# The feed-forward's input copied and shifted by DMAs, and its first two groups normalised among the attention's last slots

## The chip, the cores and the metric

The kernel runs on one core of a Trainium2 chip, as one launch. A core has TensorE (matmuls and transposes), VectorE, ScalarE and GpSimd (elementwise work) and SyncE, called SP here, which issues the DMAs. Each engine works through its own queue in order and waits on semaphores. TensorE writes its results to PSUM, eight banks of 128 partitions x 512 numbers; everything else lies in SBUF. The metric is the device time of one execution in microseconds.

## The reference, cut to what matters

Two inputs of 16 batches x 128 tokens x 128 numbers go through four stages: a cross-attention, a mixture of experts, a second cross-attention, and then six layers of local attention with a feed-forward. The change is in those six layers. Both halves of a layer begin with the same shift: of each token's 128 numbers the second 64 are taken from the token before (zeros for token 0).

```python
def shift_tokens(t):
    a, s = jnp.split(t, 2, -1)
    s = jnp.pad(s, ((0, 0), (1, 0), (0, 0)))[:, :-1]
    return jnp.concatenate([a, s], -1)

def ffn_layer(x, g, bln, W1, b1, W2, b2):
    mu = x.mean(-1, keepdims=True)
    var = ((x - mu) ** 2).mean(-1, keepdims=True)
    xn = (x - mu) / jnp.sqrt(var + 1e-05) * g + bln
    hg = xn @ W1 + b1
    a, gate = jnp.split(hg, 2, -1)
    return a * jax.nn.gelu(gate, approximate=False) @ W2 + b2
# a layer:  y = y + attn_layer(shift_tokens(y));  y = y + ffn_layer(shift_tokens(y))
```

## The kernel before

**Layout.** Y holds the running activations in SBUF as 128 tokens (partitions) x 16 batches x 128. [...]

**The attention as a pipeline.** A layer's attention has 64 units, four for each of the 16 batches. Each engine runs a list of steps, and each step has a skew: in slot c it handles unit c minus the skew. `start` writes out the first slots, `steady` is a loop over eight slots at a time, and `finish(0)` to `finish(6)` write out the last seven (slot 64 to slot 70, called finish slot 0 to 6 here). On GpSimd a slot is l_norm and l_scale of unit c-4 and l_add of unit c-3, in the order norm, add, scale; it is the scale (L555) that makes a unit ready for TensorE's transposes (l_turn_qk, L835, unit c-4). On VectorE a slot is, in this order, the split of x, the peaks of unit c-5, the sum of squares of unit c-2 (L1607), the division of unit c-6 (L1630, L1632), the small maximum of unit c-2 (L1622), the residual that writes a batch of Y (L1640, unit c-7, every fourth slot) and the rotation of unit c-1 (L1593, L1597). On TensorE a slot is scores (L854, L862), transposes of l_qk (L835), probability times values (L882), the two projections (L818, L827), output (L902), transposes of o (L892), transposes of the probabilities (L845) and, every fourth slot, those of x (L808). The engines are tied only by the semaphores between steps, so one may be slots ahead of another.

**The feed-forward.** It works in four groups g of four batches and three chunks k of the 341 hidden numbers. For each group TensorE first shifts Y into PSUM bank 1 with two matmuls against an identity and a shifted identity (shift, L923 and L924). VectorE takes the statistics from that bank (stats, L1653 and L1658), GpSimd makes 1/sqrt(var + eps) from them with an addition and a power (rstd, L566 and L568) and adds the bias b2 to Y (L571). VectorE normalises into the one buffer f_n (norm, L1666), TensorE transposes it into bank 2 (turn, L932), and ScalarE scales it into f_nT (L1227). Then come the hidden steps, written hidden(g,k) (L948, L949), the gelu on ScalarE, the gated product on VectorE (L1676), and the output (L959) with its residual (L1683).

**The order around the hand-over** is written out by hand, per engine, in into_feed_forward and out_of_feed_forward. TensorE has shift(0) behind finish slot 1, turn(0) behind slot 3, hidden(0,0) behind slot 4, shift(1) behind slot 5 and hidden(0,1) behind slot 6; VectorE has stats(0) behind slot 1, norm(0) behind slot 3, stats(1) before slot 6 and norm(1) behind it; GpSimd does all of its attention slots and only then its part of group 0. The remaining turns and shifts stand between the hidden steps of the groups before them. Between layers, the next attention's first slots are mixed into group 2 and 3, from the transpose of x at L808 on.

**SP** issues the DMAs in one queue: for each unit pair four copies that move the values across partitions (move_values, L360), for each batch two copies that bring the next batch of Y, shifted, to xin (take_x, L367 and L368), and the weights of the next layer.

Of the kernel before, what the change touches and what calls it, by code (L numbers as in the profile page):

```python
# [90 lines left out]
def build(nc, t, out):  # L91
    with ExitStack() as ctx:
# [135 lines left out]
        f_mv = sb("f_mv", [128, 4, 2])  # L228
        f_rs = sb("f_rs", [128, 4])
        f_n = sb("f_n", [128, 4, D])  # L230
# [13 lines left out]
        ld_xin = [sem(f"ld_xin{k}") for k in range(2)]  # L244
        tables, scaled_q = sem("tables"), sem("scaled_q")
# [24 lines left out]
        f = stage_sems("f_", "xs stats stat pool_st rstd n_done turned nT_done hidden gelu_done h_done out_mm yb_done "  # L270
# [4 lines left out]
        def apart(eng):  # L275


            eng.sem_inc(passed[eng.engine], 1)

# [6 lines left out]
        def _(sp):  # L286
# [87 lines left out]

            def serve_layer(ly, last):
# [50 lines left out]
        def _(pool):  # L426
# [55 lines left out]
            drive(pool, [(1, m_sum)], B, 2, 1)  # L482

# [76 lines left out]
            def feed_forward(ly, *groups):  # L560
                fb = ly * 4
                for g in groups:
                    yg = Y[:, 4 * g:4 * g + 4, :]
                    pool.wait_ge(f["stat"], upto(0, fb + g + 1))
                    apart(pool)
                    pool.tensor_scalar(f_rs[:], f_mv[:, :, 1], LN_EPS, None, ALU.add).then_inc(f["pool_st"], 1)  # L566
                    pool.wait_ge(f["pool_st"], upto(0, fb + g + 1))
                    pool.tensor_tensor(f_rs[:], f_rs[:], minus_half[:, 0:4], ALU.pow).then_inc(f["rstd"], 1)  # L568

                    pool.wait_ge(f["xs"], upto(0, fb + g + 1))  # L570
                    pool.tensor_tensor(yg, yg, f_b2[:, None, :].broadcast_to([128, 4, D]),  # L571
                                       ALU.add).then_inc(f["yb_done"], 1)

            def into_feed_forward(ly, att):
# [24 lines left out]
        def _(pe):  # L599
# [310 lines left out]
            def feed_forward(ly):  # L910
# [3 lines left out]
                def f_shift(g):  # L914

                    v = bank[:, 1, :].rearrange("p (a n) -> p a n", a=4)
                    yg = Y[:, 4 * g:4 * g + 4, :]
                    pe.wait_ge(l["res_done"], upto(0, ly * B + 4 * g + 4))
                    if g == 0:
                        pe.wait_ge(l["v_done"], upto(ub, UNITS))  # L920
                    else:
                        pe.wait_ge(f["n_done"], upto(0, fb + g))
                    pe.matmul(v[:, :, 0:HALF], ident, yg[:, :, 0:HALF], start=True, stop=True)  # L923
                    pe.matmul(v[:, :, HALF:], shift_t, yg[:, :, HALF:], start=True, stop=True).then_inc(f["xs"], 1)  # L924

                def f_turn(g):
                    pe.wait_ge(f["n_done"], upto(0, fb + g + 1))
                    if g == 0:
                        pe.wait_ge(l["qkT_done"], upto(ub, UNITS))
                    pe.wait_ge(f["nT_done"], upto(0, fb + g))  # L930
                    for n in range(4):
                        ins = pe.transpose(bank[:, 2, n * 128:(n + 1) * 128], f_n[:, n], ident)  # L932
# [30 lines left out]
                return f_shift, f_turn, f_hidden, f_out  # L963

            def into_feed_forward(ly, att):
                shift, turn_n, hidden, _ = feed_forward(ly)
# [860 lines left out]
```

## Time and profile before

| | |
|---|---|
| median of 3 runs | 2300.74 us (2296.83 to 2302.52) |
| the profiled execution's own time | 2298.88 us |
| its span, first to last instruction | 2297.1 us |
| TensorE's mean granted clock | 0.98 of full speed |
| TensorE, VectorE, ScalarE, GpSimd busy | 2163.7, 1708.3, 1555.0, 1410.4 us |
| shift matmuls, L923 and L924 | 16.0 and 14.9 us busy in all |
| GpSimd's wait ahead of L566 | 168.3 us in all, on VectorE's f_mv |

The engines work at the same time, so these busy times overlap. Busy time of TensorE is that of matmuls in a pipeline and may overlap with itself. The profiled execution is one of many, and its times are the ones that the rows further down give.

### The profile page before, as it was taken

What the parts mean: (1) busy time and instruction counts of PE and PEld (TensorE: products, weight loads), DVE (VectorE), ACT (ScalarE), POOL (GpSimd) and SP (SyncE); (2) the same over time, 40 slices, a digit from 0 to 9 for tenths busy, and PEclk for the clock granted to TensorE, in tenths of its full rate; (3) what the DMA queues carried; (4) which work ended last, traced back from release to release, by engine and by line L of the source; (5) the groups of instructions that cost most, each with busy time, mean ns of one, the idle gap of its engine ahead of it and who ended that gap; (6) DMA issues with size and microseconds to landing.
All of it is one profiled execution on the core that took longest, in us unless ns stands there. A gap on an engine that the chain in (4) does not pass through costs nothing.

```text
span 2297.1 us, 104869 instructions
## 1 busy us (share of the span) xinstructions
PE 2163.7 (94%) x36357; PEld 1677.6 (73%) x36357; DVE 1708.3 (74%) x4617; ACT 1555.0 (68%) x5192; POOL 1410.4 (61%) x2639
## 2 busy tenths in 40 slices
PE   6999789998999989999899998999989999899998
PEld 4776267776888758887588875788857888578885
DVE  4777878886888758787578875778757877578874
ACT  3553545554888748887488884888848888478883
POOL 3442711112888728887288882888828888288881
PEclk9997999997999999999999999999999999999999
DMA  3000000001211102111021110311103111021110
GB/s 102 0 0 1 0 1 0 0 0 54 75 41 42 35 26 75 40 42 35 23 77 42 41 36 18 81 42 39 39 18 79 42 40 40 16 51 43 42 40 20
DMA packets 120016, 82.33 MB, mean 36 GB/s; under 512 B 50998, under 2 KB 112580, under 8 KB 119876
## 3 DMA queue, kind: packets, MB, share of 16 engines
q1 hardware_dynamic: 119876, 80.43, 13.5%
q8 instruction: 92, 1.51, 0.3%
q14 instruction: 48, 0.39, 0.1%
HBM read 21.94 MB, written 1.05 MB: 10 GB/s over the span
## 4 chain that ended last, share of the span: by engine, by line
PE 74%; issue 5%; DVE 4%; POOL 2%; ACT 1%; DVEq 0%; POOLq 0%; ACTq 0%
PE bank L818 14%; PE bank L835 9%; PE bank L902 7%; PE bank L882 6%; PE bank L862 6%; PE bank L827 6%; PE bank L892 4%; PE bank L845 4%; PE bank L757 2%; PE bank L854 2%; PE bank L746 2%; PE bank L949 2%; PE bank L948 2%; PE bank L605 2%; PE bank L959 1%
## 5 line engine op out<-in xcount | busy, mean ns | idle before, releaser
L534 POOL TENSOR_TENSOR l_qk<-l_rot 128x512 f32<-128x512 f32 x384 | 494.2, 1287 | 106.0 <-DVE l_rot L1597 58.8
L1593 DVE TENSOR_TENSOR l_rot<-bank,l_tab 128x512 f32<-128x512 f32 x384 | 265.0, 690 | 185.7 <-ACT l_sq L1194 185.1
L1210 ACT ACTIVATE l_qkT<-bank 128x512 f32<-128x512 f32 x384 | 229.6, 598 | 255.2 <-PE bank L835 255.2
L555 POOL TENSOR_TENSOR l_qk<-l_qk,l_rn 128x512 f32<-128x512 f32 x384 | 400.7, 1044 | 0.9
L1174 ACT ACTIVATE prob<-bank,peak 128x64 f32<-128x64 f32 x1536 | 353.9, 321 | 1.3 <-DVE peak L1615 1.3
L818 PE MATMUL bank<-w_high,xs_part 128*128 128x512 f32 x768 | 347.4, 452 | 6.0 <-DVE xs_part L1584 5.4
L1597 DVE TENSOR_TENSOR l_rot<-bank,l_tab 128x512 f32<-128x512 f32 x384 | 261.4, 681 | 0.0
L1607 DVE TENSOR_REDUCE l_ss<-l_sq 128x8 f32<-128x512 f32 x384 | 259.6, 676 | 0.2
L835 PE MATMUL bank<-const,l_qk 128*128 128x128 f32 x1536 | 252.9, 287 | 6.5 <-POOL l_qk L555 5.8
L1194 ACT ACTIVATE l_sq<-bank 128x512 f32<-128x512 f32 x384 | 236.0, 615 | 23.8 <-PE bank L818 16.0
L902 PE MATMUL bank<-l_wo,l_oT 128*128 128x128 f32 x1536 | 237.4, 277 | 0.0
L827 PE MATMUL bank<-w_high,xs_part 128*128 128x256 f32 x768 | 199.9, 283 | 11.6 <-issue 11.6
L902 PEld LDWEIGHTS bank<-l_wo,l_oT 128*128 128x128 f32 x1536 | 204.8, 191 | 3.3 <-issue 0.3
L835 PEld LDWEIGHTS bank<-const,l_qk 128*128 128x128 f32 x1536 | 161.9, 141 | 42.9 <-POOL l_qk L555 9.6
L818 PEld LDWEIGHTS bank<-w_high,xs_part 128*128 128x128 f32 x768 | 144.9, 189 | 63.9 <-DVE xs_part L1584 7.1
L882 PE MATMUL bank<-l_v,probT 64*32 64x65 f32 x4608 | 177.2, 223 | 10.0 <-ACT probT L1182 6.5
L439 POOL TENSOR_SCALAR ln_rs<-ln_mv 128x1 f32<-128x1 f32 (+1 forms) x64 | 14.5, 227 | 274.2 <-DVE ln_mv L1561 129.4
L1615 DVE TENSOR_REDUCE peak<-bank 128x4 f32<-128x256 f32 x384 | 160.0, 417 | 28.9 <-PE bank L862 27.3
L862 PE MATMUL bank<-l_qkT 64*32 64x64 f32 x12288 | 174.7, 222 | 0.0
L882 PEld LDWEIGHTS bank<-l_v,probT 64*32 64x32 f32 x4608 | 115.4, 106 | 79.1 <-issue 79.1
L1632 DVE TENSOR_TENSOR o<-bank,rsum 128x256 f32<-128x256 f32 x384 | 163.0, 424 | 13.3
L882 PE MATMUL bank<-stash,probT 64*32 64x65 f32 x7680 | 172.2, 223 | 0.0
(201 smaller groups left out, 5287.8 us busy)
## 6 DMA issues: line engine op xcount, KB each, us to landing
stash<-l_v SPq DMA_DIRECT2D x768, 65.0 KB, 2.0
early<-in_L_ffn_Wqkv_dram SPq DMA_DIRECT2D x36, 256.0 KB, 3.1
l_wo<-in_L_ffn_Wo_dram SPq DMA_DIRECT2D x6, 512.0 KB, 4.0
xin<-Y SPq DMA_DIRECT2D x96, 32.0 KB
xin<-Y SPq DMA_DIRECT2D x96, 31.8 KB
f_w<-in_L_ffn_W_dram SPq DMA_DIRECT2D x6, 341.0 KB
out_dram<-X SPq DMA_DIRECT2D x4, 256.0 KB, 2.3
f_w<-in_L_ffn_W_dram SPq DMA_DIRECT2D x6, 128.0 KB
```

The source lines that it names most:

```text
L534: pool.tensor_tensor(l_qk[:, k], l_rot[:, k, 0], l_rot[:, k, 1], ALU.add).then_inc(l["add_done"], 1)
L555: pool.tensor_tensor(v, v, l_rn[:, k, :, None].broadcast_to([128, 8, L_DIM]), ALU.mult).then_inc(l["qk_done"], 1)
L818: ins = pe.matmul(bank[:, 0, :].rearrange("p (q n) -> p q n", q=2), xs_part[:, part, j // 4], w[:, 0:2, 256 * g:256 * g + 256], start=n == ...
L827: ins = pe.matmul(bank[:, 1, 0:256], xs_part[:, part, j // 4], w[:, 2, 256 * g:256 * g + 256], start=n == 0, stop=n == 2)
L835: ins = pe.transpose(bank[:, 2, n * 128:(n + 1) * 128], l_qk[:, j % 2, n * 128:(n + 1) * 128], ident)
L862: ins = pe.matmul(bank[w * WINDOW:(w + 1) * WINDOW, 3 + r, BAND * p:BAND * (p + 1)], l_qkT[rows, j % 2, queries:queries + WINDOW], l_qkT[r ...
L882: ins = pe.matmul(bank[w * WINDOW:(w + 1) * WINDOW, 6 - p, at:at + L_DIM + 1], probT[rows, j % 2, 128 * r + w * WINDOW:128 * r + (w + 1) * ...
L902: ins = pe.matmul(bank[:, 7, 256:384], l_oT[:, j // 4, p], l_wo[:, p], start=p == 0, stop=p == 7, skip_group_check=True)
L1174: ins = act.activation(prob[:, k, n * BAND:(n + 1) * BAND], bank[:, 3 + r, p * BAND:(p + 1) * BAND], ACT.Exp, bias=peak[:, k, n:n + 1])
L1593: dve.tensor_tensor(l_rot[:, k, 0].rearrange("p (q h n) -> p q h n", q=2, h=4), bank[:, 0, :].rearrange("p (q h n) -> p q h n", q=2, h=4), ...
L1597: dve.tensor_tensor(l_rot[:, k, 1].rearrange("p (q h s n) -> p q h s n", q=2, h=4, s=2), bank[:, 0, :].rearrange("p (q h s n) -> p q h s n ...
L1607: dve.tensor_reduce(l_ss[:, k, :, 0], l_sq[:].rearrange("p (h n) -> p h n", n=L_DIM), AX.X, ALU.add)\
```

## The change

The shift moves from TensorE to DMAs. The experts' buffer m_xT, which is free by then, becomes f_x, a shifted copy of all 16 batches of Y. SP fills it with two copies for each group of four batches, one of the first 64 numbers and one of the last 64 into the partition below. The copies of groups 0 to 2 are issued once batch 11's residual is done, between the moves of batch 13 and of batch 14; those of group 3 after the last residual. Row 0 of the shifted half is set to zero once. Statistics and norm read f_x. The semaphore xs and the function f_shift are gone, and the bias, which overwrites Y, now waits for the copies.

f_n, f_mv and f_rs get a second buffer (f_n's lies in c_oT, free by then), and the transposes alternate between bank 1 and bank 2. The order changes on four engines: stats, rstd and norm of groups 0 and 1 stand among finish slots 0 to 3, both turns and both copies of them behind slots 2 and 3; stats and norm of groups 2 and 3 move one group earlier.

```diff
+            def take_feed_forward(ly, first, end):
+                sp.wait_ge(l["res_done"], upto(ly * B, end))
+                apart(sp)
+                for b in range(first, end, 4):
+                    four = slice(b, b + 4)
+                    sp.dma_start(f_x[:, four, 0:HALF], Y[:, four, 0:HALF]).then_inc(ld_fx[b // 12], 16)
+                    sp.dma_start(f_x[1:, four, HALF:], Y[0:S - 1, four, HALF:]).then_inc(ld_fx[b // 12], 16)
...
                         move_values(ly, 2 * i + k, k, 1)
+                take_feed_forward(ly, 0, 12)
                 for b in range(B - 2, B):
                     for q in range(2):
                         move_values(ly, b, b % 2, q)
+                take_feed_forward(ly, 12, 16)
... GpSimd
             def into_feed_forward(ly, att):
+                rstd_n, bias = feed_forward(ly)
                 att.steady()
-                att.finish(0, 1, 2, 3)
+                att.finish(0)
+                rstd_n(0)
+                att.finish(1)
+                rstd_n(1)
+                att.finish(2, 3)
                 pool.wait_ge(ld_fw, (ly + 1) * (16 * FW_DMAS))
-                feed_forward(ly, 0)
+                bias(0)
 
             def out_of_feed_forward(ly, nxt):
-                feed_forward(ly, 1, 2, 3)
+                rstd_n, bias = feed_forward(ly)
+                rstd_n(2)
+                bias(1)
+                rstd_n(3)
+                bias(2)
+                bias(3)
... TensorE
-                att.finish(0, 1)
-                shift(0)
-                att.finish(2, 3)
+                att.finish(0, 1, 2)
+                turn_n(0)
+                att.finish(3)
+                turn_n(1)
                 pe.wait_ge(ld_fw, (ly + 1) * (16 * FW_DMAS))
-                turn_n(0)
                 att.finish(4)
                 hidden(0, 0)
-                att.finish(5)
-                shift(1)
-                att.finish(6)
+                att.finish(5, 6)
                 hidden(0, 1)
...
-                    if g < 3:
+                    if 0 < g < 3:
                         turn_n(g + 1)
                     hidden(g, 2)
...
-                    if g < 2:
-                        shift(g + 2)
... ScalarE
-                att.finish(0, 1, 2, 3)
+                att.finish(0, 1, 2)
                 act.wait_ge(ld_fw, (ly + 1) * (16 * FW_DMAS))
                 copy_n(0)
+                att.finish(3)
+                copy_n(1)
                 att.finish(4, 5)
... VectorE
-                att.finish(0, 1)
+                att.finish(0)
                 stats(0)
-                att.finish(2, 3)
+                att.finish(1)
+                stats(1)
                 norm(0)
-                att.finish(4, 5)
+                att.finish(2)
+                norm(1)
+                att.finish(3, 4, 5)
                 dve.wait_ge(ld_fw, (ly + 1) * (16 * FW_DMAS))
                 gated(0, 0)
-                stats(1)
                 att.finish(6)
-                norm(1)
...
                 for g in range(4):
-                    if 0 < g < 3:
-                        stats(g + 1)
+                    if g < 2:
+                        stats(g + 2)
...
                     if g > 0:
                         gated(g, 0)
-                    if 0 < g < 3:
-                        norm(g + 1)
+                    if g < 2:
+                        norm(g + 2)
```

## Rows read from the trace of the kernel before

**Rows 1.** The page's totals: busy time, share of the span, instructions of each engine.

```profile
PE 2163.7 (94%) x36357; PEld 1677.6 (73%) x36357; DVE 1708.3 (74%) x4617; ACT 1555.0 (68%) x5192; POOL 1410.4 (61%) x2639
```

**Rows 2.** Windows: stretch, length, busy time by engine, granted clock, DMA share, GB/s.

```profile
780.00:790.00 10.00, 10.00 (x240) 8.31 (x218) 7.91 (x22) 8.07 (x31) 8.60 (x17) 1.00 0.11 28
...
800.00:810.00 10.00, 7.87 (x124) 5.48 (x125) 3.25 (x11) 5.13 (x13) 0.00 (x0) 0.83 0.01 2
```

**Rows 3.** Timeline of GpSimd: start, us, engine, line, operation, [idle before <- releaser].

```profile
786.84 0.20 POOL L541 TENSOR_TENSOR l_t<-l_s,l_y 128x8 f32<-128x8 f32 x1
...
789.34 1.05 POOL L555 TENSOR_TENSOR l_qk<-l_qk,l_rn 128x512 f32<-128x512 f32 x1
...
792.93 1.04 POOL L555 TENSOR_TENSOR l_qk<-l_qk,l_rn 128x512 f32<-128x512 f32 x1
...
813.17 1.04 POOL L568 TENSOR_TENSOR f_rs<-f_rs,minus_half 128x4 f32<-128x4 f32 x1
```

**Rows 4.** Timeline of VectorE, finish slots 0, 1 and 3.

```profile
790.60 0.68 DVE L1597 TENSOR_TENSOR l_rot<-bank,l_tab 128x512 f32<-128x512 f32 x1
...
792.14 0.18 DVE L1630 RECIPROCAL rsum<-bank 128x4 f32<-128x4 f32 x1
...
792.70 0.16 DVE L1622 TENSOR_REDUCE l_s<-l_ss 128x8 f32<-128x16 f32 x1
...
799.39 0.18 DVE L1630 RECIPROCAL rsum<-bank 128x4 f32<-128x4 f32 x1 [0.62 <-PE bank L882]
```

**Rows 5.** Timeline of TensorE, finish slots 1 to 4.

```profile
790.89 0.66 PE L835 MATMUL bank<-const,l_qk 128*128 128x128 f32 x4
...
794.80 0.66 PE L835 MATMUL bank<-const,l_qk 128*128 128x128 f32 x4
...
798.14 0.66 PE L835 MATMUL bank<-const,l_qk 128*128 128x128 f32 x4
...
801.41 0.63 PE L932 MATMUL bank<-const,f_n 128*128 128x128 f32 x4 [0.65 <-issue]
801.87 0.28 PE L854 MATMUL bank<-l_mask,cbf 128*128 128x128 bf16 x2
```

**Rows 6.** Timeline of TensorE, the second shift and what follows it.

```profile
810.04 0.60 PE L923 MATMUL bank<-Y,const 128*128 128x256 f32 x2
...
810.91 0.61 PE L902 MATMUL bank<-l_wo,l_oT 128*128 128x128 f32 x4
```

**Rows 7.** Timeline of TensorE from hidden(0,1) to the next layer's first matmul.

```profile
811.35 1.02 PE L948 MATMUL bank<-f_nT,f_w 128*128 128x512 f32 x2
...
815.74 0.65 PE L932 MATMUL bank<-const,f_n 128*128 128x128 f32 x4 [2.51 <-DVE f_n L1666]
...
818.81 1.02 PE L948 MATMUL bank<-f_nT,f_w 128*128 128x512 f32 x2
...
820.53 2.73 PE L959 MATMUL bank<-f_w,f_h 128*128 128x128 f32 x23
...
823.21 1.02 PE L948 MATMUL bank<-f_nT,f_w 128*128 128x512 f32 x2
...
837.54 0.27 PE L808 MATMUL bank<-const,xin 128*128 128x128 f32 x1
```

**Rows 8.** Timeline of VectorE, statistics and norm of the second group.

```profile
811.23 0.89 DVE L1653 BATCH_NORM_STATS2 f_st<-bank 128x6 f32<-128x128 f32 x4 [0.88 <-PE bank L924]
...
814.24 1.36 DVE L1666 TENSOR_SCALAR f_n<-bank,f_mv,f_rs 128x128 f32<-128x128 f32 x4 [1.42 <-POOL f_rs L568]
```

**Rows 9.** Timeline of TensorE in the last layer: unit 61's transposes, and hidden(3,0).

```profile
2236.06 0.66 PE L835 MATMUL bank<-const,l_qk 128*128 128x128 f32 x4
...
2280.30 1.02 PE L948 MATMUL bank<-f_nT,f_w 128*128 128x512 f32 x2
```

**Rows 10.** SP's issues of L367: duration in ns, least, median, most.

```profile
L367 SPq DMA_DIRECT2D xin<-Y x96: 504/508/3773, 520.7 to 2201.7; - x96
```

**Rows 11.** DMA issues by line: count, KB each, median us from issue to landing.

```profile
l_wo<-in_L_ffn_Wo_dram SPq DMA_DIRECT2D x6, 512.0 KB, 4.0
```

More of the change, by code:

```diff
@@ L227, in build @@
         f_st = sb("f_st", [128, 4, 6])
-        f_mv = sb("f_mv", [128, 4, 2])
-        f_rs = sb("f_rs", [128, 4])
-        f_n = sb("f_n", [128, 4, D])
+        f_mv = sb("f_mv", [128, 2, 4, 2])
+        f_rs = sb("f_rs", [128, 2, 4])
+        f_n0 = sb("f_n", [128, 4, D])
+        f_n = (f_n0[:], c_oT[:, 1])
+        f_x = m_xT[:]
         f_nT = sb("f_nT", [128, 2, 512])
@@ L244, in build @@
         ld_xin = [sem(f"ld_xin{k}") for k in range(2)]
+        ld_fx = [sem(f"ld_fx{k}") for k in range(2)]
         tables, scaled_q = sem("tables"), sem("scaled_q")
@@ L269, in build @@
                  "add_done qk_done qk_turned qkT_done v_done o_turned oT_done out_done res_done")
-        f = stage_sems("f_", "xs stats stat pool_st rstd n_done turned nT_done hidden gelu_done h_done out_mm yb_done "
+        f = stage_sems("f_", "stats stat pool_st rstd n_done turned nT_done hidden gelu_done h_done out_mm yb_done "
                  "y_done")
@@ L278, in apart, with feed_forward_read @@
             eng.sem_inc(passed[eng.engine], 1)
+        def feed_forward_read(eng, ly, g):
+            late = g // 3
+            eng.wait_ge(ld_fx[late], (ly + 1) * (32 if late else 96))
         def one(t3, b):
@@ L482, in _ @@
             drive(pool, [(1, m_sum)], B, 2, 1)
+            pool.memset(f_x[0:1, :, HALF:], 0.0).then_inc(preset, 1)
             pool.wait_ge(ld_sc, 32)
@@ L912, in feed_forward @@
                 fb, ub = ly * 4, ly * UNITS
[L914 to L924, printed above, removed]
                 def f_turn(g):
@@ L928, in f_turn @@
                     if g == 0:
+                        pe.wait_ge(l["v_done"], upto(ub, UNITS))
+                    if g == 1:
                         pe.wait_ge(l["qkT_done"], upto(ub, UNITS))
-                    pe.wait_ge(f["nT_done"], upto(0, fb + g))
+                    pe.wait_ge(f["nT_done"], upto(0, fb + g - (g > 0)))
                     for n in range(4):
-                        ins = pe.transpose(bank[:, 2, n * 128:(n + 1) * 128], f_n[:, n], ident)
+                        ins = pe.transpose(bank[:, 1 + g % 2, n * 128:(n + 1) * 128], f_n[g % 2][:, n], ident)
                     ins.then_inc(f["turned"], 1)
@@ L961, in f_out @@
                     ins.then_inc(f["out_mm"], 1)
-                return f_shift, f_turn, f_hidden, f_out
+                return f_turn, f_hidden, f_out
             def into_feed_forward(ly, att):
-                shift, turn_n, hidden, _ = feed_forward(ly)
+                turn_n, hidden, _ = feed_forward(ly)
                 att.steady()
-                att.finish(0, 1)
-                shift(0)
-                att.finish(2, 3)
+                att.finish(0, 1, 2)
+                turn_n(0)
+                att.finish(3)
+                turn_n(1)
                 pe.wait_ge(ld_fw, (ly + 1) * (16 * FW_DMAS))
-                turn_n(0)
                 att.finish(4)
                 hidden(0, 0)
-                att.finish(5)
-                shift(1)
-                att.finish(6)
+                att.finish(5, 6)
                 hidden(0, 1)
             def out_of_feed_forward(ly, nxt):
-                shift, turn_n, hidden, output = feed_forward(ly)
+                turn_n, hidden, output = feed_forward(ly)
                 for g in range(4):
@@ L1226, in f_copy_n @@
                     act.wait_ge(f["hidden"], upto(ly * 12, 3 * (g - 1)))
-                    act.activation(f_nT[:, g % 2], bank[:, 2, :], ACT.Identity, bias=f_g[:, 1:2],
+                    act.activation(f_nT[:, g % 2], bank[:, 1 + g % 2, :], ACT.Identity, bias=f_g[:, 1:2],
                                    scale=f_g[:, 0:1]).then_inc(f["nT_done"], 1)
@@ L1648, in f_stats @@
                 def f_stats(g):
-                    dve.wait_ge(f["xs"], upto(0, fb + g + 1))
-                    v = bank[:, 1, :].rearrange("p (a n) -> p a n", a=4)
+                    feed_forward_read(dve, ly, g)
+                    v = f_x[:, 4 * g:4 * g + 4]
                     apart(dve)
@@ L1657, in f_stats @@
                     for q in range(4):
-                        ins = dve.bn_aggr(f_mv[:, q], f_st[:, q])
+                        ins = dve.bn_aggr(f_mv[:, g % 2, q], f_st[:, q])
                     ins.then_inc(f["stat"], 1)
                 def f_norm(g):
-                    v = bank[:, 1, :].rearrange("p (a n) -> p a n", a=4)
+                    v = f_x[:, 4 * g:4 * g + 4]
                     dve.wait_ge(f["rstd"], upto(0, fb + g + 1))
-                    dve.wait_ge(f["turned"], upto(0, fb + g))
+                    dve.wait_ge(f["turned"], upto(0, fb + g - (g > 0)))
                     for q in range(4):
-                        ins = dve.tensor_scalar(f_n[:, q], v[:, q], f_mv[:, q, 0:1], f_rs[:, q:q + 1],
-                                                ALU.subtract, ALU.mult)
+                        ins = dve.tensor_scalar(f_n[g % 2][:, q], v[:, q], f_mv[:, g % 2, q, 0:1],
+                                                f_rs[:, g % 2, q:q + 1], ALU.subtract, ALU.mult)
                     ins.then_inc(f["n_done"], 1)
```

20 lines of the change are left out of this document (12 added, 8 removed).

## The prediction, made before the changed kernel had run

> **What bounds the kernel now.** I read the page's engine totals first: TensorE is busy for 94% of the span, more than any other engine [rows 1]. That is an average over stages, so next come windows of ten microseconds at the first hand-over from attention to feed-forward. Up to 790 us TensorE is full and GpSimd is at 8.60 of 10; from 800 us TensorE is at 7.87 and GpSimd at nothing [rows 2]. In the attention, then, two engines are nearly full, in slots of about 3.6 us; in the feed-forward nothing is full and waits set the time. The third view is the timeline of each engine, to be read with slot numbers, because the engines don't do the same slot at the same moment. At 786.84 GpSimd is done with finish slot 0 (unit 60 scaled) and starts on unit 61, slot 1 [rows 3]. VectorE ends its slot 0, whose last instruction is the rotation of unit 63, at 790.60 + 0.68 = 791.28 [rows 4]. GpSimd is 4.4 us, more than a slot, ahead of VectorE, and TensorE uses that lead: unit 61 is scaled by 789.34 + 1.05 = 790.39, and its transposes run at 790.89 [rows 3, 5].
>
> **What the change removes.** (a) Four pairs of shift matmuls a layer, each 0.87 us (810.04 to 810.91) [rows 6]. Two of them, behind slots 1 and 5, stand ahead of the second hidden step. (b) The feed-forward's waits on one buffer. TensorE starts hidden(0,1) at 811.35 and reaches the first matmul of the next layer at 837.54, 26.19 us later [rows 7]. In it stands an idle stretch of 2.51 us before the transposes at 815.74: VectorE's norm at 814.24 had waited 1.42 us on GpSimd's rstd [rows 7, 8].
>
> The same stretch for the new order, from hidden(0,1) as zero: a hidden step takes 1.72 us (818.81 to 820.53), an output group 2.68 (820.53 to 823.21), a turn 0.46 (801.41 to 801.87) [rows 5, 7]. VectorE can begin stats(2) at about 0.5, when slot 6's residual is done. From the start of bn_stats to the end of GpSimd's power is 814.21 - 811.23 = 2.98 us [rows 3, 8], so rstd(2) stands at 3.5; norm(2) takes 1.36 us [rows 8], the gated product behind it (128x512 like GpSimd's and VectorE's other passes) about 0.7: gated(0,1) is done at 5.7. TensorE has finished hidden(0,2) by 3.4 and waits until 5.7. Then hidden(1,0), output(0), hidden(1,1), turn(2), hidden(1,2), hidden(2,0), output(1), hidden(2,1), turn(3), hidden(2,2): six times 1.72, twice 2.68, twice 0.46 are 16.6 us. VectorE stays ahead (a group needs 1.3 for the weights, 3.0 for statistics and power, 1.4 for norm, three times 0.7 and the residual 0.7, some 8.5, beside 8.3 on TensorE with a step in hand). The stretch is 22.3 us instead of 26.19: 3.9 us gained.
>
> **What it adds to GpSimd's queue, and who waits.** GpSimd calls rstd_n(0) right behind its slot 0 and rstd_n(1) behind its slot 1. Queued behind the first are norm, add and scale of units 61 to 63, which TensorE's slots 1 to 3 need. stats(0), which rstd_n(0) waits for, is queued on VectorE behind VectorE's slot 0. Before, rstd stood behind all four slots, where nothing of the attention was left.
>
> First wait: VectorE is free at 791.28; plus 2.98 us, GpSimd resumes at 794.26, where it now starts unit 61 at 786.84 [rows 3, 4, 8]: 7.42 us late. TensorE had 0.50 us in hand (790.39 to 790.89), and I allow 0.1 for the semaphore, so its transposes of unit 61 start at 797.9, 7.0 us late.
>
> Second wait: rstd_n(1) needs stats(1), behind VectorE's slot 1, whose division of unit 59 needs the value products that TensorE does after the transposes of unit 61, just held up. From GpSimd's end of scaling unit 61: 0.1 to the transposes; 1.25 to VectorE's reciprocal (798.14 to 799.39, where VectorE waited for exactly this); 0.72 to the end of the small maximum (792.14 to 792.86); 2.98 to GpSimd [rows 3, 4, 5, 8]. That is 5.05 us more. GpSimd is now 12.5 us late: unit 62 is scaled at 792.93 + 1.04 + 12.5 = 806.45, and its transposes start at 806.55 instead of 794.80 [rows 3, 5].
>
> From there TensorE itself is last. Slot 2 takes 3.34 us (794.80 to 798.14) and turn(0) at its end 0.46, so unit 63 is turned at 810.35; GpSimd has it ready at about 809. From 798.14 to slot 4 at 801.87 it took 3.73 us, with 0.65 idle ahead of the turn at 801.41 [rows 5]. A turn stays there (turn(1) now), the idle goes: 3.08, slot 4 begins at 813.43. Slots 4 and 5 took 9.48 us to hidden(0,1) and lose one shift: 8.6, so hidden(0,1) starts at 822.05. Plus 22.3: the next layer's first matmul at 844.35 instead of 837.54, **6.8 us later**. Layers 2 to 5 have the same queue orders, and I take them alike. In the last layer there is no next one; its transposes of unit 61 and its hidden(3,0) stand at 2236.06 and 2280.30, 44.24 us apart [rows 9]; the new distance is 844.35 - 790.89 = 53.46: 9.2 us later.
>
> **The clock.** Behind the stretch where TensorE waited, the granted clock is 0.83 in 800 to 810 us [rows 2]. The levels are 2.4 and 1.2 GHz, so 3.4 us of the ten were at the low one, and at most half of that, 1.7 us, was lost; since part of such a stretch is waiting anyway I price one at 1.0 us. One is in the sum already (it lies in the 9.48). TensorE's idle stretches of now 7.0 us and, from slot 2's scores at 801.0 to 806.55, 5.6 us are longer than any here: I add half a stretch, 0.5 us a layer. Bounds: -1.0 (none at all) to +3 (three more).
> The Trainium skill says, in "TensorE: Matmul & The Clock Gate" under "HAM oscillation — how this bites in real kernels", that waits between bursts of matmuls throttle the array again, so that each burst starts cold. The trace agrees in direction, by the 0.83 above. Taken at its word, slot 1 and slot 2 would both start at the low clock, which is the second rival below.
>
> **The copies.** SP issues six behind the moves of batch 13 and ahead of those of batch 14. An issue of such a copy takes 0.508 us in the median [rows 10], 3 us in all; batch 14's values are ready two slots, 7.2 us, after batch 13's, so nothing queues. Each copy is 128 KB, 768 KB together; 512 KB land in 4.0 us [rows 11], so I estimate 6 to 8 us, against three slots (10.8 us) until the moved values of batch 14 are read, and some seven slots until stats(0). The last two copies start when slot 6's residual is done and should land 4 us later; stats(3) is due after 7. Bounds: 0 to 6 us a layer, if they held up batch 14's moves by their whole landing; I take 0, the windows showing a DMA share of 0.11 [rows 2]. Statistics and norm now read SBUF instead of a bank; the trace has these two only from the bank (1.36 us for the norm), and I bound the difference at 0 to 0.3 us less a group and take 0. The memset of 1024 elements on one partition stands once, ahead of a stage boundary: GpSimd passes 512 a partition in 1.04 us [rows 3], so 0 to 2.1 us; I take 0, since the tables it delays are read a stage later.
>
> **Sum.** 5 x 6.8 + 9.2 = 43.2; clock 6 x 0.5 = 3.0; together +46.2 us. The profiled execution took 2298.88 us (span 2297.1, and 1.8 around it), so 2345.1; the median of the three runs is 1.9 us above it: **2347 us**.
>
> **Rivals.**
> *The second wait is hidden*, VectorE reaching stats(1) before it is asked for: six times 5.05 less, 2317 us. Against it: the division comes ahead of stats(1) in program order.
> *The low clock takes over*: three more slow stretches a layer instead of half, 6 x 2.5 = +15, 2362 us. For it: idle stretches of 7 us; against it: after 806 TensorE is fed without a break.
> *The copies hold up batch 14's values* by the upper bound, 6 x 6 = +36: 2383 us. Against it: the 10.8 us in hand.
> *The other side: GpSimd's lead covers rstd.* If the statistics were there when GpSimd asks, only gains were left: two shifts 1.74, the idle 0.65, the stretch 3.9, less 0.46 for turn(1), 5.8 us a layer and 3.4 in the last: 2300.7 - 32 = 2268 us. It decides from where both waits together cost TensorE less than 5.8 us; I find 12.6. Against it are two rows: 786.84 and 790.60.
> *Waits and gains cancel*: waits of 5.8 us a layer leave the last layer's 2.4 and the clock's 3.0, 2306 us.
>
> **Chances.** Forecast 0.66, low clock 0.12, second wait hidden 0.08, copies 0.05, other side 0.05, cancelling 0.04. The range is 2316 to 2374: down to the case of the second wait hidden, up to the clock's upper bound and its error, not to the copies' worst. What this measurement can't tell from no change is 0.3%, 7 us. Slower 0.92, same 0.03, faster 0.05.
>
> **What would show it.** Right: GpSimd idle for about 6.0 us on VectorE's f_mv ahead of a layer's first rstd and 3.7 us ahead of its second; TensorE's transposes of l_qk idle for 7.0 and 5.6 us a layer with GpSimd's l_qk as releaser; about 22 us from hidden(0,1) to the next layer's first matmul. Wrong: the transposes of unit 61 less than 2 us behind where they were; VectorE's statistics waiting on a DMA; the stretch after hidden(0,1) still near 26 us.

## The result, and the profile after

The changed kernel takes 2455.86 us in the median (2453.11 to 2458.78), the kernel before 2299.35 us beside it: ratio 1.0677, 95% interval 1.0658 to 1.0696. It is 156.5 us slower. The prediction had the direction, but its 2347 us and its range up to 2374 us lie far below.

The page of the kernel after, the engine totals (they answer to [rows 1]), two groups of part 5 and three of part 6 (there: size of one, median us from issue to landing, which is absent for some):

```profile
PE 2186.4 (89%) x36261; PEld 1692.9 (69%) x36261; DVE 1720.5 (70%) x4617; ACT 1555.4 (63%) x5192; POOL 1412.1 (57%) x2640
...
L918 PE MATMUL bank<-l_v,probT 64*32 64x65 f32 x4608 | 181.4, 227 | 73.7 <-DMA stash<-l_v 61.4
L871 PE MATMUL bank<-const,l_qk 128*128 128x128 f32 x1536 | 258.8, 292 | 71.0 <-POOL l_qk L576 70.7
...
l_wo<-in_L_ffn_Wo_dram SPq DMA_DIRECT2D x6, 512.0 KB, 9.7
m_xT<-Y SPq DMA_DIRECT2D x24, 128.0 KB
m_xT<-Y SPq DMA_DIRECT2D x24, 127.0 KB
```

No engine has more to do (TensorE 96 instructions less, GpSimd one more); busy times grow by at most 23 us, and the waits have grown. Two of them stand out on TensorE: 73.7 us ahead of L918 (probability times values), 61.4 of it for a DMA that moves values, and 71.0 us ahead of L871 (transposes of l_qk), 70.7 of it for GpSimd. The prediction has the second and not the first. Windows of the first hand-over (start:end, length, busy us of TensorE, its weight load, VectorE, ScalarE, GpSimd, granted clock, DMA share, GB/s; they answer to [rows 2]):

```profile
780.00:790.00 10.00, 0.29 (x3) 0.05 (x1) 0.87 (x2) 1.41 (x5) 2.51 (x4) 0.64 0.23 53
800.00:810.00 10.00, 3.48 (x84) 2.80 (x83) 5.08 (x18) 2.96 (x11) 4.26 (x8) 0.84 0.11 28
```

From 780 to 790 us TensorE stands still, while the DMA engines are busy for 0.23 of their time. The timeline of SP's queue tells why (start, duration of the issue):

```profile
763.74 0.70 SPq L390 DMA_DIRECT2D m_xT<-Y  x1
764.49 0.80 SPq L391 DMA_DIRECT2D m_xT<-Y  x1
765.33 6.44 SPq L390 DMA_DIRECT2D m_xT<-Y  x1
771.81 0.70 SPq L391 DMA_DIRECT2D m_xT<-Y  x1
772.56 6.87 SPq L390 DMA_DIRECT2D m_xT<-Y  x1
779.47 0.69 SPq L391 DMA_DIRECT2D m_xT<-Y  x1
780.49 24.92 SPq L369 DMA_DIRECT2D stash<-l_v  x16
```

L390 is the copy of the first 64 numbers (128 partitions), L391 the shifted one (127 partitions). An issue that follows an L391 takes 6.4 or 6.9 us instead of 0.7. The six issues hold the queue from 763.74 to 780.16; the prediction had 3 us. Batch 14's moves (L369) stand behind them, and the first of the 16 that the last row adds up, with the pauses between them, is held up too, behind the third L391:

```profile
780.49 6.65 SPq L369 DMA_DIRECT2D stash<-l_v  x1
```

The other 15 take 0.5 to 0.6 us each. So it is three long issues, not two, that delay batch 14's values, the last one to 787.14. A fourth stands behind the last group's L391: the next layer's weights (L342) take 6.16 us to issue at 838.09, and in the median they land 9.7 us after their issue instead of 4.0 [rows 11]. TensorE's timeline has the waits of this layer (in brackets: idle us before it, and what ended them; they answer to [rows 5]), and GpSimd's the two ahead of the additions for rstd ([rows 3]):

```profile
790.60 0.28 PE L918 MATMUL bank<-l_v,probT 64*32 64x65 f32 x1 [10.31 <-DMA stash<-l_v]
...
810.05 1.12 PE L871 MATMUL bank<-const,l_qk 128*128 128x128 f32 x4 [6.57 <-POOL l_qk L576]
...
819.08 1.12 PE L871 MATMUL bank<-const,l_qk 128*128 128x128 f32 x4 [4.83 <-POOL l_qk L576]
```

```profile
805.29 0.23 POOL L588 TENSOR_SCALAR f_rs<-f_mv 128x4 f32<-128x4 f32 x1 [5.99 <-DVE f_mv L1682]
...
814.17 0.38 POOL L588 TENSOR_SCALAR f_rs<-f_mv 128x4 f32<-128x4 f32 x1 [4.18 <-DVE f_mv L1682]
```

The 10.31 us are new to the prediction and cost six layers 61.4 us. The other two waits are the predicted ones. The last group's shifted copy is late as well: issued at 836.96, it lands 9.39 us later by the chain of waits, where 4 us were predicted, and the statistics of group 3 wait for it (a row of that chain, then VectorE's timeline; [rows 8] has them from the bank):

```profile
836.96 9.39 DMA m_xT<-Y
...
846.50 0.87 DVE L1677 BATCH_NORM_STATS2 f_st<-m_xT 128x6 f32<-128x128 f32 x4 [2.77 <-DMA m_xT<-Y]
```

### The profile page after: what moved, and what is told of

It is laid out like the page before. It is cut to its first block, busy times and chain, and to the rows that moved or that the text cites. A ratio compares the mean times of both kernels' runs of the same rounds, so it can differ in the third digit from the quotient of the medians.

```text
span 2456.9 us, 104739 instructions
## 1 busy us (share of the span) xinstructions
PE 2186.4 (89%) x36261; PEld 1692.9 (69%) x36261; DVE 1720.5 (70%) x4617; ACT 1555.4 (63%) x5192; POOL 1412.1 (57%) x2640
## 4 chain that ended last, share of the span: by engine, by line
PE 67%; SPq 7%; issue 5%; DVE 3%; POOL 3%; DMA 2%; ACT 2%; POOLq 0%; DVEq 0%; ACTq 0%
PE bank L854 12%; PE bank L871 8%; PE bank L938 6%; PE bank L918 6%; PE bank L863 5%; PE bank L898 5%; SPq L390 4%; PE bank L928 3%; PE bank L881 3%; SPq L369 2%; PE bank L985 2%; PE bank L793 2%; PE bank L974 2%; PE bank L975 2%; PE bank L890 2%
## 5 line engine op out<-in xcount | busy, mean ns | idle before, releaser
L871 PE MATMUL bank<-const,l_qk 128*128 128x128 f32 x1536 | 258.8, 292 | 71.0 <-POOL l_qk L576 70.7
L938 PE MATMUL bank<-l_wo,l_oT 128*128 128x128 f32 x1536 | 245.4, 284 | 2.8 <-ACT l_oT L1238 2.8
L918 PE MATMUL bank<-l_v,probT 64*32 64x65 f32 x4608 | 181.4, 227 | 73.7 <-DMA stash<-l_v 61.4
L871 PEld LDWEIGHTS bank<-const,l_qk 128*128 128x128 f32 x1536 | 166.1, 144 | 107.9 <-POOL l_qk L576 74.4
L918 PEld LDWEIGHTS bank<-l_v,probT 64*32 64x32 f32 x4608 | 118.4, 108 | 145.4 <-issue 145.4
L938 PEld LDWEIGHTS bank<-l_wo,l_oT 128*128 128x128 f32 x1536 | 210.8, 197 | 8.1 <-ACT l_oT L1238 4.3
L1654 DVE RECIPROCAL rsum<-bank 128x4 f32<-128x4 f32 x384 | 69.0, 180 | 168.6 <-PE bank L918 167.3
L918 PE MATMUL bank<-stash,probT 64*32 64x65 f32 x7680 | 176.4, 227 | 0.7 <-issue 0.7
## 6 DMA issues: line engine op xcount, KB each, us to landing
xin<-Y SPq DMA_DIRECT2D x96, 31.8 KB
```

The lines of the kernel that those rows point to most:

```text
L871: ins = pe.transpose(bank[:, 2, n * 128:(n + 1) * 128], l_qk[:, j % 2, n * 128:(n + 1) * 128], ident)
L918: ins = pe.matmul(bank[w * WINDOW:(w + 1) * WINDOW, 6 - p, at:at + L_DIM + 1], probT[rows, j % 2, 128 * r + w * WINDOW:128 * r + (w + 1) * ...
L938: ins = pe.matmul(bank[:, 7, 256:384], l_oT[:, j // 4, p], l_wo[:, p], start=p == 0, stop=p == 7, skip_group_check=True)
```

## Experiments

Three causes were to be told apart: the copies, the rstd calls between GpSimd's slots, and TensorE's low clock. Ratios are to the kernel before, run on the same chip beside each, with their 95% intervals.

### The copies: cut the 127 partitions

`e1_split127` is the kernel after with each shifted copy issued as two, of 112 and 15 partitions:

```diff
-            eng.wait_ge(ld_fx[late], (ly + 1) * (32 if late else 96))
+            eng.wait_ge(ld_fx[late], (ly + 1) * (48 if late else 144))
...
-                    sp.dma_start(f_x[1:, four, HALF:], Y[0:S - 1, four, HALF:]).then_inc(ld_fx[b // 12], 16)
+                    for r, n in ((0, 112), (112, 15)):
+                        sp.dma_start(f_x[r + 1:r + 1 + n, four, HALF:], Y[r:r + n, four, HALF:]).then_inc(ld_fx[b // 12], 16)
```

> The changed kernel with one edit: each shifted copy of 127 partitions is issued as two, of 112 and of 15 partitions. Theory A (a copy over 127 partitions is worked off by one DMA engine, whose queue fills and holds SP): the issues of L390 fall from a median of 3.6 us to under 1 us, TensorE's 61 us of waits on stash<-l_v go, stats(3) no longer waits for a DMA, and with fewer low-clock stretches the time falls by 6 x 14, to about 2372 us (2360 to 2390). Rival B (the number of 256-byte pieces is what costs, whichever engine takes them): nothing moves, 2445 to 2460 us.

Measured: 2369.17 us, 1.0298 (1.0270 to 1.0327), 86.7 us less than the kernel after, 14.4 a layer. SP's issues of the copy of the first 64 numbers (least, median, most in ns), first of the kernel after, then of this one, and this one's landing of the piece of 112:

```profile
L390 SPq DMA_DIRECT2D m_xT<-Y x24: 662/3570/6870, 763.7 to 2410.4; - x24
```

```profile
L390 SPq DMA_DIRECT2D m_xT<-Y x24: 662/686/722, 765.3 to 2326.7; - x24
...
m_xT<-Y SPq DMA_DIRECT2D x24, 112.0 KB, 2.4
```

The same bytes in one more issue a group, and the stalls are gone: 6870 ns at most become 722, and 112 KB land in 2.4 us. The largest part of the loss was the shape of one DMA. What the copy keeps busy can be read from the windows of 766 to 772 us, first in the kernel after, where SP is held in one issue until 771.77, then in e1 (the last two numbers are DMA share and GB/s):

```profile
766.00:772.00 6.00, 6.00 (x131) 5.11 (x123) 4.70 (x14) 5.44 (x22) 5.44 (x9) 1.00 0.08 17
```

```profile
766.00:772.00 6.00, 6.00 (x159) 4.81 (x158) 5.04 (x13) 4.79 (x19) 4.95 (x12) 1.00 0.47 101
```

A share of 0.08 of the core's 16 DMA engines is 1.3 engines' worth, 0.47 is 7.5. At 17 GB/s the 127 KB take 7.6 us, an estimate from this row, and the long issues begin 7.23 us apart (765.33 and 772.56).

`e5_copies_alone` is the kernel before plus the six copies of batches 0 to 11 a layer. Nobody reads them; the bias waits for them, since it overwrites Y. `e6_copies_alone_split` is the same with 112 and 15:

```diff
+                for b in range(first, end, 4):
+                    four = slice(b, b + 4)
+                    sp.dma_start(f_x[:, four, 0:HALF], Y[:, four, 0:HALF]).then_inc(ld_fx, 16)
+                    sp.dma_start(f_x[1:, four, HALF:], Y[0:S - 1, four, HALF:]).then_inc(ld_fx, 16)
...
+                take_feed_forward(ly, 0, 12)
...
+                    pool.wait_ge(ld_fx, (ly + 1) * 96)
```

> The kernel before, with nothing but the six copies of batches 0 to 11 added on SP behind the moves of batch 13 (nobody reads them; the bias on GpSimd waits for them, as it must). Theory A: SP is held for about 15 us, the moves of batch 14 are late, TensorE waits some 10 us a layer on stash<-l_v and loses 1 to 2 us more to the clock: 2299 + 6 x 12 = 2370 us (2355 to 2385). Rival (the copies only hurt together with the new order): under 2310 us.

> As the run with the copies alone, with the shifted copies in pieces of 112 and 15 partitions. Theory A: nine short issues, nothing held, 2299 to 2306 us. Rival B (the number of 256-byte pieces): as without the split, about 2370 us.

Measured: 2376.1 us, 1.0328 (1.0292 to 1.0364), for the one; 2299.81 us, 0.9997 (0.9980 to 1.0015), for the other. The group of probability times values in the first:

```profile
L895 PE MATMUL bank<-l_v,probT 64*32 64x65 f32 x4608 | 179.1, 225 | 71.7 <-DMA stash<-l_v 61.6 <-ACT probT L1195 6.6 <-issue 1.8
```

The wait of 61.6 us is the one of the kernel after (61.4). So the six copies cost 76.0 us by themselves, 12.7 a layer, and their bytes, cut otherwise, cost nothing that can be told. It takes neither the new order nor a reader.

Is it the misaligned or unequal partitions, the length, or the number 127? `e11_pieces_113_14` and `e12_pieces_126_1` are the same kernel with other pieces. 113 is a prime like 127; 126 is nearly as long as 127, and 14 divides it. The edit of e11 against e6, where e12 has `((0, 126), (126, 1))`:

```diff
-                    for r, n in ((0, 112), (112, 15)):
+                    for r, n in ((0, 113), (113, 14)):
```

> The run with the copies alone, split, but with pieces of 113 and 14 partitions instead of 112 and 15 (113 is prime, 112 is 7 x 16). Divisor theory (a copy is spread over as many DMA engines as divide its number of partitions, at most 16, so 113 stays on one): nearly as slow as unsplit, 6 x 11 over before, 2365 us (2350 to 2380), with long issues again. Rival (it is the full length of 127 rows, or the last partition, that is slow): 2300 us like 112 and 15.

> The same with pieces of 126 and 1 partitions (126 is 9 x 14). Divisor theory: 14 engines share it, 2297 to 2306 us, issues under 1 us. Rival (any number that is not a multiple of 16 falls on one engine): about 2370 us.

Measured: 2370.81 us, 1.0289 (1.0259 to 1.0319), with 113; 2301.86 us, 1.0005 (0.9994 to 1.0016), with 126. SP's issues, of the one and of the other:

```profile
L385 SPq DMA_DIRECT2D m_xT<-Y x36: 723/3239/5822, 764.7 to 2284.0; - x36
```

```profile
L385 SPq DMA_DIRECT2D m_xT<-Y x36: 661/800/992, 765.5 to 2217.1; - x36
```

A smaller prime is nearly as bad as 127, a longer composite as good as 112. So it isn't the length, the last partition or the multiple of 16. Both slow numbers are odd and prime, both fast ones are even: that it goes by the largest divisor, and not by odd and even, these four don't show; an odd composite of this length, such as 117, wasn't run.
The Trainium skill says this in "DMA: Bandwidth & Descriptors", under "Why a DMA increments its semaphore by 16 and not by 1": the copy is shared among the largest number of DMA engines, up to 16, that divides its slowest dimension, and 127 partitions go to one. The four runs agree, and so does the share of 0.08 above.

### The order on GpSimd

`e2_rstd_late` is the kernel after with both rstd calls behind the four finish slots; `e3_split_and_late` is that on top of e1:

```diff
-                att.finish(0)
+                att.finish(0, 1, 2, 3)
                 rstd_n(0)
-                att.finish(1)
                 rstd_n(1)
-                att.finish(2, 3)
```

> The changed kernel with one edit: on GpSimd rstd_n(0) and rstd_n(1) stand behind finish slots 0 to 3, everything else as changed. The queue theory of the prediction: GpSimd's waits of 6.0 and 4.2 us ahead of the rstd go, TensorE's waits for l_qk of unit 61 and 62 go, VectorE waits some 2 us for rstd ahead of norm(0), net 8 to 10 us a layer less: 2400 us (2390 to 2415). Rival (the waits only change places, because TensorE is held by the DMAs and by VectorE's norm anyway): 2440 to 2460 us.

> The changed kernel with both edits: shifted copies in 112 and 15 partitions, and rstd_n(0), rstd_n(1) behind GpSimd's finish slots 0 to 3. If the two costs are separate and nothing else is left, their savings add: 2456 - 87 - 52 = 2317 us. Theory A has them overlap less, since only the gains and VectorE's wait for rstd ahead of norm(0) (about 3 us with the norm itself) are then left: 2299 - 6 x 5.8 + 6 x 3 = 2283 us; I expect 2280 to 2300. Rival (something third in the new order costs too): above 2310 us.

Measured: 2403.84 us, 1.0449 (1.0419 to 1.0478), 52.0 us less than after; and 2318.73 us, 1.0082 (1.0064 to 1.0100), 50.4 us less than e1, 8.4 a layer. The two edits save 138.7 and 137.1 us, added apart (86.7 + 52.0) and done together: they are two separate costs. GpSimd's order is the second.

e3 was expected at 2280 to 2300 us and is still slower than before: something third costs too, as the expectation's rival had it. Its timelines (VectorE and TensorE):

```profile
799.26 1.11 DVE L1689 TENSOR_SCALAR f_n<-m_xT,f_mv,f_rs 128x128 f32<-128x128 f32 x4 [3.13 <-POOL f_rs L591]
```

```profile
801.36 0.41 PE L927 MATMUL bank<-const,o 128*128 128x128 f32 x2 [2.31 <-DVE o L1655]
```

The same fault, one engine on: VectorE's norm(0) waits 3.13 us for rstd with the division of the next slot behind it, and TensorE waits 2.31 us for that division.

### TensorE's low clock

`e7_fill_stalls` is e1 with 48 needless transposes of the identity on TensorE ahead of the two late transposes. They write into the bank in which the output matmuls accumulate, and some of the output is changed, other than the expectation below says; the order of the work isn't.

```diff
+                    if isinstance(u, int) and u in (61, 62):
+                        for _ in range(48):
+                            pe.transpose(bank[:, 7, 0:128], ident, ident)
                     pe.wait_ge(l["qk_done"], upto(ub, u + 1))
```

> The split run (2369 us) with 48 more transposes of the identity into an unused part of a bank ahead of TensorE's transposes of units 61 and 62, that is in the two places where it waits for GpSimd; they stand for about 5 us of work each in a wait of 6.6 and 4.9 us and leave the result alone. Clock theory (the slots behind the waits run at the low clock and cost 2 to 3 us a layer): 2369 - 6 x 2.5 = 2354 us (2345 to 2362). Rival (the low clock lies only in waits and costs nothing): 2369 us or up to 10 more, if the filler overruns the second wait.

Measured: 2346.44 us, 1.0200 (1.0185 to 1.0216): 22.7 us less than e1, 3.8 a layer, by giving TensorE more to do. The windows of e1, then of e7:

```profile
780.00:800.00 20.00, 13.41 (x321) 10.99 (x327) 12.12 (x34) 10.31 (x40) 11.17 (x21) 0.88 0.12 31
800.00:820.00 20.00, 13.19 (x279) 10.69 (x264) 7.26 (x29) 8.97 (x31) 7.40 (x14) 0.78 0.01 2
```

```profile
780.00:800.00 20.00, 18.52 (x350) 15.94 (x350) 12.42 (x40) 10.82 (x41) 10.04 (x18) 1.00 0.11 28
800.00:820.00 20.00, 17.11 (x327) 13.56 (x326) 7.81 (x26) 9.45 (x27) 7.41 (x14) 1.00 0.01 3
```

The number behind GpSimd's is the granted clock. Between the levels of 2.4 and 1.2 GHz, a mean of 0.88 means (1 - 0.88) x 20 / 0.5 = 4.8 us at the low one, and 0.78 means 8.8 us. Each gap's slot starts low in e1: the transposes behind the waits take 1.11 and 1.12 us (the lines are shown further down), the same ones in e7 what they took before, 0.66 us [rows 5]:

```profile
797.33 0.66 PE L875 MATMUL bank<-const,l_qk 128*128 128x128 f32 x4 [1.19 <-POOL l_qk L577]
...
805.66 0.65 PE L875 MATMUL bank<-const,l_qk 128*128 128x128 f32 x4
```

With the gaps filled both windows are at 1.00 (the next, 820 to 840 us, is at 0.91 in e7 and 1.00 in e1, so a little is given back).

### Towards a better order

`e4_norm_later` is e3 with norm(0) and norm(1) a slot later, and the turns and their copies too:

```diff
... VectorE
                 stats(1)
-                norm(0)
                 att.finish(2)
+                norm(0)
+                att.finish(3)
                 norm(1)
-                att.finish(3, 4, 5)
+                att.finish(4, 5)
```

> As the run with both edits, and besides the norms of groups 0 and 1 one slot later on VectorE (behind slots 2 and 3), and turn(0), turn(1) and their copies behind slots 3 and 4. VectorE then has no wait for rstd in its attention slots. Theory A: the gains alone, 2299 - 33 = 2266 us (2260 to 2278). Rival (the gains were never there, the new order only moves waits behind hidden(0,1)): 2290 to 2300 us.

Measured: 2285.11 us, 0.9940 (0.9925 to 0.9956), 33.6 us less than e3, 5.6 a layer, and the first version faster than before. What e3's lines suggested is borne out in direction; of the 2260 to 2278 us expected it falls short.

`e8_gated_first` puts VectorE's gated product (0,1) ahead of norm(2):

```diff
+                    if g == 0:
+                        gated(0, 1)
                     if g < 2:
                         norm(g + 2)
...
-                    gated(g, 1)
+                    if g > 0:
+                        gated(g, 1)
```

> As the run with the norms later, and VectorE does the gated product (0,1) ahead of norm(2). In the split run TensorE waited 2.65 us for that product ahead of hidden(1,0). If that wait is what ends last, 6 x 2.65 less than with the norms later: about 2251 us. Rival (norm(2) and what follows it are late instead, turn(2) or hidden(2,0) wait): no change to within 4 us.

Measured: 2284.45 us, 0.9931 (0.9917 to 0.9944). Against e4 the intervals overlap: no gain that can be told, so the rival holds and not the 2251 us expected.

`e9_bias_early` takes the bias passes of GpSimd away from the norms of groups 2 and 3:

```diff
                 bias(0)
+                bias(1)
+                bias(2)
...
                 rstd_n(2)
-                bias(1)
                 rstd_n(3)
-                bias(2)
+                pool.wait_ge(f["n_done"], upto(0, ly * 4 + 4))
                 bias(3)
```

> As the run with the gated product first (2284 us), with GpSimd's biases of groups 1 and 2 right behind that of group 0, and that of group 3 behind norm(3): no 128x512 addition of GpSimd stands beside norm(2) or norm(3). Contention theory (VectorE's norm from SBUF to SBUF stands still while GpSimd adds the bias; four norm instructions took 1.11 us alone, 1.96 and 2.94 us beside it): they take 1.1 to 1.4 us again, hidden(1,0)'s and hidden(2,0)'s waits shrink, 6 x 1 to 2 us less: 2275 us (2270 to 2281). Rival (the long norms wait for something else, or another wait takes over): 2281 to 2287 us.

Measured: 2272.93 us, 0.9887 (0.9872 to 0.9902), 11.5 us less than e8, as expected, and 1.1% faster than before, the best version. VectorE's norm(2) and norm(3), in e4 and then in e9, each time with GpSimd's bias passes (L596) near them:

```profile
814.05 1.27 POOL L596 TENSOR_TENSOR Y<-Y,f_b 128x512 f32<-128x512 f32 x1
814.21 1.96 DVE L1688 TENSOR_SCALAR f_n<-m_xT,f_mv,f_rs 128x128 f32<-128x128 f32 x4 [1.68 <-POOL f_rs L591]
...
821.52 2.49 POOL L596 TENSOR_TENSOR Y<-Y,f_b 128x512 f32<-128x512 f32 x2
821.67 2.93 DVE L1688 TENSOR_SCALAR c_oT<-m_xT,f_mv,f_rs 128x128 f32<-128x128 f32 x4 [0.25 <-POOL f_rs L591]
```

```profile
813.72 1.11 DVE L1689 TENSOR_SCALAR f_n<-m_xT,f_mv,f_rs 128x128 f32<-128x128 f32 x4
...
819.67 1.11 DVE L1689 TENSOR_SCALAR c_oT<-m_xT,f_mv,f_rs 128x128 f32<-128x128 f32 x4 [1.03 <-POOL f_rs L591]
...
820.96 1.27 POOL L596 TENSOR_TENSOR Y<-Y,f_b 128x512 f32<-128x512 f32 x1 [1.41 <-DVE c_oT L1689]
```

`e10_spread` takes e9 and spreads VectorE's part over more slots: stats(0) behind slot 1, norm(0) behind 2, stats(1) behind 3, norm(1) behind 4, and TensorE's turn(1) behind 5. On GpSimd rstd(1) goes behind bias(0), so that bias(0) follows rstd(0) directly:

```diff
... GpSimd
                 rstd_n(0)
-                rstd_n(1)
                 pool.wait_ge(ld_fw, (ly + 1) * (16 * FW_DMAS))
                 bias(0)
+                rstd_n(1)
                 bias(1)
... VectorE
-                att.finish(0)
+                att.finish(0, 1)
                 stats(0)
-                att.finish(1)
-                stats(1)
                 att.finish(2)
                 norm(0)
                 att.finish(3)
+                stats(1)
+                att.finish(4)
                 norm(1)
```

> As the run with the biases early, and the hand-over spread out: VectorE has stats(0) behind slot 1 as in the kernel before, norm(0) behind slot 2, stats(1) behind slot 3, norm(1) behind slot 4; turn(0) behind slot 3, turn(1) behind slot 5. In the run with the norms later, TensorE waited 1.55 us in slot 1 for VectorE's division, which stats(0) had pushed back, and went to the low clock. If that is what is left of the missing gain: 6 x 2 less, about 2263 us. Rival (stats(1) and norm(1) in slots 3 and 4 cost as much there): no change to within 4 us.

Measured: 2289.11 us, 0.9954 (0.9940 to 0.9967), 16.2 us more than e9. My theory fell. VectorE's and TensorE's lines:

```profile
796.87 2.05 DVE L1689 TENSOR_SCALAR f_n<-m_xT,f_mv,f_rs 128x128 f32<-128x128 f32 x4 [1.70 <-POOL f_rs L591]
```

```profile
799.90 0.66 PE L928 MATMUL bank<-const,o 128*128 128x128 f32 x2 [2.08 <-DVE o L1655]
```

With the statistics a slot later, norm(0) comes too close behind them: it waits 1.70 us for rstd, takes 2.05 us beside a bias pass, and TensorE waits 2.08 us for the division behind it. That accounts for part of the loss: counted from the transposes of unit 60 (786.36, in e9 786.86), the first layer reaches the next one 2.3 us later than in e9 (832.63 and 830.84). norm(0) takes 1.97 to 2.05 us in all six layers, but each of the next four layers is 3.3 to 6.5 us longer than in e9, in two profiled executions that lie 25.0 us apart where the medians lie 16.2; what else is in that is open.

## Why the prediction was wrong, step by step

**"The copies" is the step that failed.** It said "nothing queues" and "I take 0"; it was 86.7 us, 14.4 a layer, above even its upper bound of 6. Its rows were the wrong ones. [rows 10] is the issue of a copy of 128 partitions, [rows 11] a load of 512 KB into 128 partitions, and I scaled by bytes alone. Half of the new copies have 127 partitions, and by the spacing of the long issues they are worked off one after the other at some 7 us each, where 6 to 8 us were estimated for all six. The issue time was low even without a stall: 0.66 to 0.80 us, not 0.508. Of [rows 10]'s figures the median of 508 ns was taken; the last, 3773 ns, was not asked after. SP's timeline of the kernel before has that issue right behind a shifted copy of 31.8 KB and 127 partitions, L368:

```profile
521.30 0.79 SPq L368 DMA_DIRECT2D xin<-Y  x1
522.14 3.77 SPq L367 DMA_DIRECT2D xin<-Y  x1
```

A maximum seven times the median, in the very row that carried the price, was worth a question, but it would not have given the answer: weights were queued ahead of this one, and the five other issues of L367 that directly follow an L368 take 0.85 to 0.87 us. That a copy of 127 partitions and four batches stalls what follows it, no row of the kernel before shows. The rival that had the mechanism, batch 14's values held up, got 0.05 and 36 us.

**The first and second wait held.** GpSimd idle 5.99 and 4.18 us (6.0 and 3.7 predicted); TensorE's transposes of l_qk idle 6.57 and 4.83 us (7.0 and 5.6), released by GpSimd's l_qk. In the kernel after the copies shift all absolute times, so e1 is the one to hold against the sum. It has these lines of TensorE:

```profile
798.69 1.11 PE L872 MATMUL bank<-const,l_qk 128*128 128x128 f32 x4 [6.58 <-POOL l_qk L577]
...
807.68 1.12 PE L872 MATMUL bank<-const,l_qk 128*128 128x128 f32 x4 [4.86 <-POOL l_qk L577]
...
824.28 1.02 PE L975 MATMUL bank<-f_nT,f_w 128*128 128x512 f32 x2
...
830.53 1.13 PE L975 MATMUL bank<-f_nT,f_w 128*128 128x512 f32 x2 [2.65 <-DVE f_h L1701]
...
847.93 0.27 PE L845 MATMUL bank<-const,xin 128*128 128x128 f32 x1
```

Absolute times of two executions don't start alike: the transposes of unit 60, which no edit touches, stand at 787.29 in the kernel before and at 788.43 in e1, 1.1 us later. With that taken off, unit 61 is at 797.55 (predicted 797.9), unit 62 at 806.54 (806.55), hidden(0,1) at 823.14 (822.05) and the next layer at 846.79 (844.35): 9.3 us later than before instead of 6.8. The two waits put units 61 and 62 where they were predicted, to 0.4 us; what is missing comes behind them. "I take them alike" was too low as well: from one layer's first matmul to the next one's the four layers that follow are 11.2 to 13.8 us longer than before (299.9 to 302.5 us against 288.6 to 289.7).

**The clock was mis-sized.** The sum has 0.5 us a layer, with an upper bound of 3; filling the gaps gave back 3.8. The prediction took one low stretch of 3.4 us from [rows 2] and added half of one. In e1 the stretches at 1.2 GHz are 4.8 + 8.8 = 13.6 us by the windows above: four times the one stretch, since the slot behind each wait starts low. The rival of the low clock (2362 us) came nearest for this part: e1, which has the waits and no slow copies, took 2369.
The Trainium skill's rule cited for that rival, bursts that each start cold ("TensorE: Matmul & The Clock Gate", "HAM oscillation — how this bites in real kernels"), is what e1 (1.11 and 1.12 us for the transposes behind the waits) and e7 (0.66 and 0.65 us) show. The rival's 2.5 us a layer would have been the better price, though still below 3.8.

**The stretch behind hidden(0,1)** was predicted at 22.3 us and is 23.65 in e1: the gated product comes 0.55 us later than worked out (6.25 instead of 5.7), the rest 0.8 longer. The norms fit that: norm(2), ahead of that product, takes 1.96 us in e1 where the sum has 1.36, and norm(3) 2.93 us, both beside GpSimd's bias. In the kernel after it is 28.2 (835.68 to 863.86), longer than the 26.19 of before; e1, which differs in the copies alone, has 23.65. So there the late copies lost even the part that the change was to win.

**The sum.** e7, with neither slow copies nor low clock in its gaps, is 45.5 us slower than before (2346.44 - 2300.91); the sum had 43.2 for the same thing. Its parts don't agree as well: hidden(0,1) came 1.1 us earlier than predicted (820.76, in an execution that stands 0.2 us early at unit 60), the stretch was 2.4 longer (24.67). That the total fits is then partly luck. The whole of it: 86.7 (copies) + 22.7 (clock) + 45.5 (order of GpSimd and VectorE, less the gains) = 154.9; the 1.6 us left are what the medians of the kernel before differ by in the two sets (2299.35 and 2300.91).

**Statistics and norm from SBUF** were taken as equal, with at best 0.3 us to gain. Alone, the norm does gain that (1.11 us against 1.36 [rows 8]). Beside GpSimd's bias it loses up to 1.8 us in e4 and 2.3 in e9, a case that the bounds left out.

**What stays open:** e4 and e9 still have an idle stretch of 1.55 us on TensorE ahead of the transposes of o, with VectorE's statistics between its slots; e10 didn't remove them at a profit, and no other place was tried.

## What to carry to other kernels

Before a DMA is priced by its bytes, look at its partition count: a token shift by one makes 127 of 128, and cutting that copy in two was worth 86.7 us here, where the pieces mattered: 112 and 15 or 126 and 1 cost nothing, 113 and 14 nearly as much as 127. Count what its queue still has to issue behind it. A step that waits for another engine doesn't belong between slots of a pipeline in which its own engine has only a slot of lead; and where a row carries a price, ask what its maximum is.

## What the runs showed of the hardware

**A copy's issue can block its queue.** One shifted copy of 127 partitions took SP no longer than others to issue (0.69 to 0.80 us); it was the issue directly behind it that took 6.1 to 6.9 us, whatever it was: a copy of 128 partitions, a move of values or a load of weights, in all six layers. The stall shows on the wrong line.

**GpSimd's pass holds up VectorE's norm from SBUF.** The norm of 4 x 128x128 from SBUF takes 1.11 us alone, 1.96 us with one bias pass of 128x512 beside it and 2.93 us with two (e4); moving the passes brought back 1.11 and, in the whole, 11.5 us. The passes themselves take 1.26 to 1.28 us with or without a norm beside them. In e9 norm(1) has three passes beside it and takes 3.41 us (800.02 to 803.43; the passes 799.38 to 803.10). Before, the norm read PSUM, and a bias pass at 814.18 did not stretch the one at 814.24 ([rows 8]: 1.36 us); all 24 norms of that kernel take 1.35 to 1.37 us.
The Trainium skill has this in "SBUF — State Buffer", "Who interferes with whom": the two share one pair of ports, and a scalar operation on VectorE from SBUF to SBUF can, in one of its modes, take it whole; whichever engine comes first keeps it for its whole instruction and the other waits. The durations agree for the order that these runs have, the pass ahead of the norm (814.05 and 814.21 in e4).

**A wait can cost more than its length.** 11.4 us of waiting in a layer of e1 (6.58 + 4.86) cost another 3.8 us in clock, since the work behind them started at 1.2 GHz.
